# Straight-line attention with two exponentials per unit instead of looped attention with three

## The reference

```
q = (x @ Wq + bq) / sqrt(16)        16 heads of 16 features, all 2048 rows together
k, v = cond @ Wkv + bkv             2048 keys for every query
q, k, v = fake-quantised to 127 levels
attn = softmax(q @ k.T)             per head, 2048 x 2048
attn = clip(round(attn / s), 0, 255) * s,   s = max(attn) / 255 per row
out = (attn @ v) @ Wp + bp
```

## Time and profile before

| | us |
|---|---|
| median of 3 executions (2227.49 to 2244.91) | 2234.46 |
| the profiled execution | 2242.98 |
| its span, first to last instruction | 2241.2 |
| attention, from the barrier before to the barrier behind it | 1202.5 to 2046 |

### The profile page before, as it was taken

One profiled execution on the slowest core, in us unless ns is written; L12 is line 12 of the kernel. 1 busy time (PEld: TensorE's weight loads), 2 busy tenths in 40 slices (PEclk: granted clock), 3 DMA queues, 4 the chain that ended last, 5 costly groups with the idle time before them and its releaser, 6 DMA issues. The chain is left out here.

```text
span 2241.2 us, 42040 instructions
## 1 busy us (share of the span) xinstructions
PE 1832.4 (82%) x12368; PEld 1273.1 (57%) x12514; DVE 1682.5 (75%) x2852; ACT 1673.6 (75%) x2987; POOL 527.5 (24%) x433
## 2 busy tenths in 40 slices
PE   6888999999999999999676667666676666664999
PEld 5776878777777777777453322222222222232887
DVE  5885676867777777777886888888878887886443
ACT  4667888888888888888368888888888887895211
POOL 2002555555555555555100000000000000002001
PEclk8998999999999999999899998899888998997999
DMA  4000000000000000000814998888888887896000
GB/s 133 15 5 29 0 28 0 28 0 28 0 28 0 28 0 28 0 28 0 174 26 83 167 166 156 154 164 164 160 152 160 161 163 150 161 166 145 10 10 19
DMA packets 566191, 173.18 MB, mean 77 GB/s; under 512 B 535168, under 2 KB 558592, under 8 KB 566144
## 3 DMA queue, kind: packets, MB, share of 16 engines
q1 hardware_dynamic: 566144, 172.57, 38.1%
HBM read 27.83 MB, written 2.10 MB: 13 GB/s over the span
## 5 line engine op out<-in xcount | busy, mean ns | idle before, releaser
L1278 ACT ACTIVATE levels<-s_ps,nb,qstep 128x512 int16<-128x512 f32 (+1 forms) x768 | 696.8, 915 | 118.8 <-DVE nb L1215 115.4
L1145 PE MATMUL s_ps<-kT,qT 128*128 128x512 bf16 x1451 | 492.0, 429 | 266.6 <-ACT levels L1278 253.4
L1204 DVE TENSOR_REDUCE mx<-s_ps 128x1 f32<-128x512 f32 (+1 forms) x768 | 636.6, 864 | 69.0 <-PE s_ps L1145 49.6
L603 DVE SCALAR_TENSOR_TENSOR xs<-x_ps,cw,xs 128x508 f32<-128x508 f32 (+2 forms) x393 | 291.1, 741 | 174.3 <-ACT xs L525 135.9
L1145 PEld LDWEIGHTS s_ps<-kT,qT 128*128 (+1 forms) x1532 | 117.7, 101 | 513.8 <-issue 488.5
L494 PE MATMUL o_ps<-wo,hid 128*128 x1024 | 242.9, 380 | 4.9 <-DVE acc L590 4.9
L659 POOL TENSOR_TENSOR hid<-y,sg 128x512 f32<-128x512 f32 x128 | 175.4, 1371 | 277.5 <-ACT sg L547 184.8
L1505 POOL MEMSET minus_half_o<- 128x4 f32 x1 | 0.1, 102 | 962.8 <-POOLq L1087 962.8
L494 PEld LDWEIGHTS o_ps<-wo,hid 128*128 128x128 f32 x1024 | 192.7, 189 | 39.5 <-issue 9.8
L1155 PEld LDWEIGHTS ao_ps<-vi,levels_T 128*128 128x128 f16 x4096 | 145.7, 98 | 82.7 <-issue 35.9
L525 ACT ACTIVATE xs<-x_ps,cb,cw 128x512 f32<-128x512 f32 x131 | 101.8, 777 | 116.5 <-PE x_ps L446 116.4
(11 more groups left out here) (200 smaller groups left out, 3220.5 us busy)
## 6 DMA issues: line engine op xcount, KB each, us to landing
w_raw<-winT_dram SPq DMA_DIRECT2D x18, 512.0 KB, 4.4
wo_raw<-woutT_dram SPq DMA_DIRECT2D x9, 512.0 KB, 5.7
kT<-zeros SPq DMA_DIRECT2D x4, 1024.0 KB, 19.4
qT<-zeros SPq DMA_DIRECT2D x4, 1024.0 KB, 16.0
levels_T<-levels SPq DMA_TRANSPOSE x256, 4.3
acc<-xT_dram SPq DMA_DIRECT2D x4, 512.0 KB, 6.1
w_bc<-winT_dram SPq DMA_DIRECT2D x16, 128.0 KB, 2.4
acc<-x_dram SPq DMA_DIRECT2D x1, 2048.0 KB, 11.5
```

The lines of the kernel that those rows point to most:

```text
L603: dve.scalar_tensor_tensor(to, x_ps[:, :, 0:SEQ - s], cw[:, head, TAPS - 1 - s], to, ALU.mult, ALU.add).then_inc(chain if s < TAPS - 1 els ...
L1145: return pe.matmul(s_ps[:, BANKS[h % 2][chunk], :], qT[:, bass.ds(round_, 1), h % NH, :].rearrange("p b t -> p (b t)"), kT[:, h % NH, at:a ...
L1204: dve.tensor_reduce(mx[:, h % 2, at:at + 1], src, AX.XY if what == "cd" else AX.X, ALU.max).then_inc(max_done, 1)
L1278: act.activation(levels[:, s, at:at + banks * GT].rearrange("p (c k) -> p c k", c=banks), s_ps[:, bank:bank + banks, :], ACT.Exp, bias=nb[ ...
```

## The change

- All loops over blocks are gone: 256 units are written out on every engine, with constant semaphore counts and addresses, and the increments of `held` are gone.
- Two exponentials per unit: one over a and b, which lie in neighbouring banks (1024 wide), and one over c and d. PE waits once, for `ab_exp`, before the score a of the next unit and the three scores b of the one after it.
- The steps of all blocks are made at once at the start: three instructions over 256 columns.
- The sum of the two partial sums and its reciprocal (as a power of -1) are made by GpSimd, once a block, into `rtot`. `finish` on DVE is one instruction, and waits for `tot_ready` too.
- `sums` has two slots of blocks; ACT waits for `tot_ready` at the start of a block before it reuses one.

```diff
 # PE, step n
-    pe.wait_ge(a_exp, n + 1)
-    pe.sem_inc(held, 1)
-    score(qt, h + 1, "a").then_inc(a_ready, 1)
-    pe.wait_ge(b_exp, n + 1)
-    pe.sem_inc(held, 1)
-    for _ in range(2):
-        score(qt, h + 2, "b")
-    score(qt, h + 2, "b").then_inc(b_ready, 1)
+    pe.wait_ge(ab_exp, n + 1)
+    score(n + 1, "a").then_inc(a_ready, 1)
+    for _ in range(2):
+        score(n + 2, "b")
+    score(n + 2, "b").then_inc(b_ready, 1)
 # DVE
     dve.wait_ge(nb_ready, n)
-    dve.sem_inc(held, 1)
     dve.wait_ge(max_done, n * 3 + 3)
-    dve.sem_inc(held, 1)
     dve.tensor_tensor_reduce(low, mx, shift, nstep, ..., nb).then_inc(nb_ready, 1)
...
-    if h == NH - 1 and exists(qt, h, 1):
-        steps(qt + 1)
+# once, ahead of all units: nstep, reciprocal, shift over [P, BATCH, NH]
 # finish
-    dve.wait_ge(pv_done, last * NH + NH)
-    dve.tensor_tensor(ab_sum, both[..., 0], both[..., 1], ALU.add)
-    dve.tensor_tensor(tot, ab_sum, both[..., 2], ALU.add)
-    dve.reciprocal(rtot, tot)
+    dve.wait_ge(tot_ready, qt + 1)
+    dve.wait_ge(pv_done, (qt + 1) * NH)
     dve.tensor_tensor(att[qt], o_ps, rtot, ALU.mult).then_inc(scaled, 1)
 # ACT
     act.wait_ge(nb_ready, n + 1)
-    exps(n, qt, h, "a", a_exp)
-    exps(n, qt, h, "b", b_exp)
-    exps(n, qt, h, "cd", cd_exp)
+    if n % NH == 0 and n >= 2 * NH:
+        act.wait_ge(tot_ready, n // NH - 1)
+    exps(n, "ab", ab_exp)
+    exps(n, "cd", cd_exp)
+# POOL, once a block
+    pool.wait_ge(cd_exp, (qt + 1) * NH)
+    pool.tensor_tensor(tot, sums[:, qt % 2, :, 0], sums[:, qt % 2, :, 1], ALU.add)
+    pool.tensor_tensor(rtot[:, qt % 2, :], tot, minus_one, ALU.pow).then_inc(tot_ready, 1)
```

More of the change, by code:

```diff
@@ L1110, in attention @@
         turned = [sem(f"at_turned{i}") for i in range(RING)]
         block = ctx.enter_context(nc.Block())
[L1113 to L1122, removed]
         @block.sync
         def _(sp):
[L1126 to L1137, removed]
+            for n in range(UNITS):
+                s = n % RING
+                sp.wait_ge(cd_exp, n + 1)
+                if n >= RING:
+                    sp.wait_ge(pv_done, n - RING + 1)
+                sp.dma_start_transpose(lT[:, s, :, :].bitcast(F16), levels[:, s, :].bitcast(F16)).then_inc(turned[s], 16)
@@ L1139, in _, with score @@
         @block.tensor
         def _(pe):
-            def score(qt, h, chunk):
-                round_ = qt if h < NH else qt + 1
+            def score(n, chunk):
+                qt, h = divmod(n, NH)
                 at = KEYS[h % 2][chunk]
[L1145 to L1152, removed]
-                pe.sem_inc(held, 1)
+                return pe.matmul(s_ps[:, BANKS[h % 2][chunk], :], qT[:, qt, h, :], kT[:, h, at:at + GT],
+                                 start=True, stop=True)
@@ new lines, in _ @@
+            score(0, "b").then_inc(b_ready, 1)
+            score(0, "c")
+            score(0, "d").then_inc(cd_ready, 1)
+            score(0, "a").then_inc(a_ready, 1)
+            score(1, "b").then_inc(b_ready, 1)
+            score(1, "c")
+            score(1, "d").then_inc(cd_ready, 1)
+            for n in range(UNITS):
+                if n + 1 < UNITS:
+                    pe.wait_ge(ab_exp, n + 1)
+                    score(n + 1, "a").then_inc(a_ready, 1)
+                if n + 2 < UNITS:
+                    for _ in range(2):
+                        score(n + 2, "b")
+                    score(n + 2, "b").then_inc(b_ready, 1)
+                if n >= LAG:
+                    if n % NH == LAG and n >= NH:
+                        pe.wait_ge(scaled, n // NH)
+                    values(n - LAG)
+                if n + 2 < UNITS:
+                    pe.wait_ge(cd_exp, n + 1)
+                    score(n + 2, "c")
+                    score(n + 2, "d").then_inc(cd_ready, 1)
@@ L1195, in _, with maxima @@
+            for n in range(UNITS - LAG, UNITS):
+                values(n)
         @block.vector
         def _(dve):
-            def maxima(n, h, what):
-                bank = BANKS[h % 2]
+            def maxima(n, what):
+                u = n % 2
+                bank = BANKS[u]
                 ready, at, src = {"b": (b_ready, 0, s_ps[:, bank["b"], :]),
@@ L1203, in maxima, with bias @@
                 dve.wait_ge(ready, n + 1)
-                dve.tensor_reduce(mx[:, h % 2, at:at + 1], src, AX.XY if what == "cd" else AX.X,
+                dve.tensor_reduce(mx[:, u, at:at + 1], src, AX.XY if what == "cd" else AX.X,
                                   ALU.max).then_inc(max_done, 1)
-            def bias(n, h):
-                u = h % 2
-                if not (isinstance(n, int) and n == 0):
+            def bias(n):
+                u = n % 2
+                qt, h = divmod(n, NH)
+                if n:
@@ L1217, in bias @@
                                          nb[:, u:u + 1]).then_inc(nb_ready, 1)
[L1219 to L1233, removed]
@@ L1249, in body @@
[L1249 to L1253, removed]
-                    if h == NH - 1 and exists(qt, h, 1):
-                        steps(qt + 1)
-                    if h == LAG and exists(qt, 0, -1):
-                        finish(qt, qt - 1)
-                    if exists(qt, h, 1):
-                        maxima(n + 1, h + 1, "cd")
-                        maxima(n + 1, h + 1, "a")
-                        bias(n + 1, h + 1)
@@ new lines, in _ @@
+            dve.tensor_scalar(nstep[:, :, :], qstep[:, :, :], -1.0, None, ALU.mult).then_inc(step_chain, 1)
+            dve.wait_ge(step_chain, 1)
+            dve.reciprocal(shift[:, :, :], nstep[:, :, :]).then_inc(step_chain, 1)
+            dve.wait_ge(step_chain, 2)
+            dve.tensor_scalar(shift[:, :, :], shift[:, :, :], LN255, None, ALU.mult).then_inc(step_chain, 1)
+            dve.wait_ge(step_chain, 3)
+            for n in range(UNITS):
+                maxima(n, "b")
+                if n % NH == LAG + 1 and n >= NH:
+                    finish(n // NH - 1)
+                maxima(n, "cd")
+                maxima(n, "a")
+                bias(n)
@@ L1271, in _ @@
+            finish(BATCH - 1)
         @block.scalar
         def _(act):
[L1273 to L1282 removed]
```

113 lines of the change are left out of this document (41 added, 72 removed).

## The result

The changed kernel took 2148.85 us (median of 4, 2146.64 to 2153.54); the kernel before, run beside it, 2235.36 us. The ratio is **0.9614, 95% interval 0.9573 to 0.9655**: 3.9% faster, where 3.5% was forecast. The profiled execution took 2153.54 us, its span 2151.8; that of before 2242.98 and 2241.2.

The account below looks back on a forecast made before the run. Bound: a circle over two units (5.86 us), after the change one unit through bank 3 (2.87). Stage 732 + 4.5 + 7.5 + 6 = 750 us for 830; with +1.5 and -0.7, minus 79: median 2155, range 2110 to 2207.

Parts of the forecast that it names:

- three circles: Chains of waits between engines in attention: one unit through bank 3 2.57 us, DVE alone 2.76, c and d 5.86 over two units.
- The circle of one unit: Bias, exponential, score a, its maximum, next bias, through bank 3: from 2.57 to 2.87 us, taking over as the bound.
- gap before `bias`: DVE's wait between the maximum of a and `bias`: 0.19 us before, 0.15 taken after, bounds 0.03 and 0.19.
- rival 1: Late wait sits on the instruction, POOL disturbs nobody: 2.75 us a unit, minus 118, median 2117; chance 0.15.
- DVE alone: DVE's step from one bias to the next when nothing is late: 2.76 us before, 2.72 after.
- Straight code at nothing for its fetches: Fetching the written-out code costs 0; the range allows 0.3 us for each of some 50 refills of PE's code, 15 us.
- finish: DVE's end of each block, cut to the scaling alone: costs 0.3 us beyond DVE's slack, 15 times, 4.5 us.
- GpSimd's port: POOL's sum and power on SBUF shut out `bias` on DVE: 0.5 us a block, 7.5 us, between 0 and 44.
- The clock: Units at the lower clock level in attention: 31 us before, 6 kept, between 0 and 31, as long units go.
- Rival 5: Clock locks into 3.50 us a unit, every second unit at the lower level: plus 75, median 2309; chance 0.06.
- The start: Steps of all blocks made at once before the first bias, reciprocal 1.75 us: plus 1.5 us, uncovered.
- floor near 2.6: DMA turns of 512 KB take 2.44 us at the best 215 GB/s, so 2.6 us a unit would be hard.

Follow-up runs that it names:

- late-wait version: The changed kernel with the two waits of `bias` swapped, so that the one for `max_done` is written first: 2121.13 us, ratio 0.9479.
- score b once: The changed kernel with one score b a unit instead of three equal ones, same output: 2202.85 us, ratio 0.9848.

## Why the prediction was right, point by point

- **What bounds: right.** It named three circles within 0.4 us and said that the merged exponential shortens one and lengthens the other. Three exponentials (5.75 a pair for 5.74 by its terms), the late wait (2.77 for 2.75) and the cut into a and b, c, d (3.236 for 3.24) each moved the time by the sum along a circle. The late wait alone would not tell the circle from DVE's own work, since the gap is part of both. The score b once does (a score longer by 0.24 us, a unit by 0.22), and so does the other cut, with DVE's and ACT's work as before.
- **The circle of one unit: 2.87, measured 2.88.** Its open term was the gap before `bias`, 0.15 between 0.03 and 0.19: it was 0.14. PE's wait was 0.05 for 0.07, and the score 0.39 for 0.38. The choice of 0.15 over 0.03 is 31 of the 38 us between the forecast and rival 1 (the rest is the port's 7.5), and rival 1's 2117 came as the late-wait version's 2121. It was a choice and not derived: no row said which of the two waits would be the one of its own, and in this the forecast had some luck. The Trainium skill (VectorE: DVE Perf Modes, "The DRAIN you can't avoid") says that in a chain of VectorE copies the semaphore costs nothing extra. The traces here show for another instruction that the wait's form costs: 0.03 us with the late wait on the instruction, 0.14 with it as one of its own, 0.19 with an increment besides. Two small slips changed nothing: DVE alone was 2.75 us by its own two times, not 2.76, and the chances of faster by over 1% add up to 0.905, not 0.88.
- **Straight code at nothing for its fetches: right in size.** Four single units are 0.25 us longer, in blocks 7, 8, 9 and 11: 1 us where up to 15 was allowed for. The same units have them in the run with score b once, so it is nothing random. The trace of the changed kernel shows where the time goes:

```profile
1545.75 0.22 DVE L1186 CUSTOM_DVE_ANT_0 low<-mx,shift,nstep 128x3 f32<-128x3 f32 x1
1546.15 0.08 DVE L1186 DVE_READ_ACCUMULATOR2_ANT nb<- 128x1 f32 x1 [0.18 <-issue]
```

In each of the four the read behind `bias` starts 0.40 us after it and not 0.15. The four lie exactly 128 recorded instructions of VectorE apart, and 1.1 to 1.6 us behind each of these biases a transfer of 8 KB of instructions starts. That points at VectorE's code, where the prediction priced PE's. It is not the fetch alone: in the late-wait version the same four places come in time, and the cause stays open.

- **finish: 0.16 us a block, 0.3 predicted.** 0.33 us of DVE's time meets a slack of some 0.17 in the unit. Over 15 blocks 2.4 for 4.5.
- **GpSimd's port: 7.5 us predicted, 0 measured.** The step that costed it by the earlier trace rows failed: that row is a sum over 1024 columns, and neither a power nor a sum over 16 columns held a bias up. The Trainium skill (SBUF — State Buffer, "SBUF: two separate sides") has the one that starts second wait for the other's whole instruction. The runs agree for sums over 256 columns (0.68 for 0.22 us), and for the power they don't: 48 of them, twelve in a row, left every bias beside them alone.
- **The clock: 6 us predicted, under 1 measured,** and the reason given holds as far as long units go: the low stretches went from 170.7 to 78.5, 54.6 and 6.2 us as the longest units became shorter and fewer, and came back to 41.0 with 0.5 us more in `finish`. It is not the whole of it. Rival 5's lock did not come in this kernel, but with the score b once it did, with no long unit at all, and not at its price: 3.10 us a unit and not 3.50, since only the score on the circle is slowed. That edit takes work from PE and adds idle time at once, so the run doesn't tell whether the idle time that the prediction named is what counts.
- **The start:** 1.5 predicted, some 1.3 measured; the reciprocal over 256 columns took 1.753 us for 1.75. POOL's power took 2.91 us, and its sum 0.21.
- **DMA:** 183 GB/s predicted, 181 measured; the turns land in 4.5 us, as before. The late-wait version moved on at 2.77 us a unit, so the floor near 2.6 was not met and stays untested.

The sum for the stage was 750 and is 738: 255 x 2.879 = 734.1, finish 2.4, long units 1, the first block 0.5. So the port, the clock and `finish` were all sized too high, by 7.5, 5.6 and 2.1 us, and the units a little too low. The forecast's minus 79 against the profiled minus 89.4 (minus 86.5 by the medians) is these 12 us, and small ones outside.

## What to carry to other kernels

Where buffers are handed round between engines, write each circle out as a sum, per unit, before you weigh any engine's load: an instruction merged off an engine busy for 86% gained nothing here until another circle was shortened, then 12 us, and the same instructions cut the other way lost 5%. When an instruction has two waits, write first the one that is met late, so that it sits on the instruction, and the one long met becomes an instruction of its own: 0.11 us a unit, 28 us in this kernel, for a swap of two lines. And after a change that shortens units, look at the clock's records: a good part of a gain here (5.6 of the stage's 13.1 us from GpSimd's sums) came from slow stretches that went with the longest units.

## What the runs showed of the hardware

- The granted clock stayed at 0.50 for all 791 us with four score matmuls a unit, and at 1.00 with six, while a unit grew only from 2.88 to 3.10 us. The useful work was the same.
- A `finish` longer by 0.5 us, once in 47 us, brought 35 us more at the lower clock.
- Instructions of GpSimd on SBUF operands behave unlike beside VectorE: sums over 256 columns, 0.61 us each, stretched a bias threefold (0.22 to 0.68 us); sums over 16 columns, 0.21 us, and powers over 16 columns, 2.89 us each, not at all.
- Of two waits written ahead of a VectorE instruction the second was an instruction of its own (255 times in each of two kernels). With the late one there, the gap before the bias is 0.14 us, and 0.03 with the early one there.
- ACT, over two banks and over three, takes 1.20 and 1.62 us, and 0.78 over one: some 0.42 us for each further bank of 512.
